# Self-attention of a decoder layer: GpSimd adds the last two keys' weighted values onto the first two, TensorE sums 14 terms per batch instead of 16

## The chip, the cores and the metric

One core of one Trainium2 chip runs the whole kernel. The metric is the device time of the kernel in microseconds (us). All times of the trace come from one profiled execution, and places in it are microseconds from the start of its span.

## The reference

One decoder layer over `x` of shape 32 x 128 x 128 (32 batches, 128 positions, D = 128): self-attention, cross-attention and a mixture of 8 experts of which each position takes two, each followed by a residual and a layer norm. The change touches the self-attention, whose 16 heads of 8 numbers attend to each other within one position:

```python
q = bitlinear(x, wq).reshape(B, S, H, Dh)      # k and v alike
scores = jnp.einsum('bshd,bstd->bsht', q, k) / Dh ** 0.5
attn = jax.nn.softmax(scores, axis=-1)         # over the 16 keys t of the same position
ctx = jnp.einsum('bsht,bstd->bshd', attn, v)
ctx = jnp.swapaxes(ctx, 1, 2).reshape(B, S, D)
return bitlinear(ctx, wo)
```

So a position has 16 x 16 scores, and its context is a sum over 16 keys of exponential times value, divided by the sum of the exponentials. `bitlinear` rounds its input to 8 bits after an rms norm and its weights to -1, 0, 1.

## The kernel before

**Stages.** The self-attention runs first, up to about 205 us; the cross-attention and the experts follow, and its last pieces (the output projection, residual and norm of the last tiles) run between the first pieces of the cross-attention. The self-attention takes one batch (128 positions on 128 partitions) per slot; four batches are a tile `u`, slots `j` = 0 to 3. `turns` writes out the slots of tiles 0 and 1, then a hardware loop over tiles 2 to 7 (two tiles a turn); the slots of the tail are written out by hand. Each engine runs its own list in a fixed order, and semaphores join the lists.

**One batch.** In slot `k` the engines work on different batches:

- TensorE multiplies batch k into `PS` with `w_pairs`, which holds for each pair of heads the sum of a query and a key weight, and into values. ScalarE squares the result into `pair_sq` (two buffers) and copies the values to `v1` (four buffers).
- VectorE's `pair_scores` reduces the squares of batch k-1 to scores, subtracts the key part and each head's largest, and writes `S1d` (lines 1962 to 1972). In slot 0 it does `largest_y` between the halves of this reduction, in slot 1 `y_scale` (`inv` and `s2`, lines 1948 and 1950), which waits for `clip2_ready` from GpSimd's `y_stats`.
- ScalarE's `exponentials` of batch k-2 (line 1449) writes the exponentials into the last 16 columns of each of the 16 key rows of `prod2` (two buffers of 16 x 144 floats; `TC` = 128 + 16). It waits for the scores and for the sum two batches before, which read the same buffer.
- GpSimd's `weigh` of batch k-2 (line 797) multiplies each key's exponentials with its values into the first 128 columns of that key's row, and raises `av_prod`.
- TensorE's `sum_keys` of batch k-3 (line 1033) adds the 16 rows of 144 columns in bank 6 of `PS`: 16 matmuls with the identity in fp32, which the trace shows as 32 passes. It waits for `av_prod` and for `hctx_ready` of the batch before, because the bank is single.
- VectorE's `context` of batch k-4 takes the reciprocal of the summed exponentials (line 1936) and scales the sum into `hctx` (line 1939), at the head of its slot, ahead of `pair_scores`. SyncE then stores `hctx` to `shuffle` and reads it back transposed into `Y`.

**Around it.** Per tile, GpSimd has three small pieces besides `weigh`, in this order: in slot 0, behind `weigh`, `y_stats` (lines 805 to 813: rms of `Y` and its clip); in slot 1, ahead of `weigh`, `y_rows` (lines 775 and 776), which waits for `s2` from `y_scale`; in slot 3, ahead of `weigh`, `first_scales` (lines 782 to 788), which waits for `mv1` from VectorE's `add_x` in slot 2. In tiles 0 and 1 it also centres expert weights (line 732) and takes powers of the rms of `x` (line 702). Its steps that read what it has just written wait on the engine's own chain counter (`ch`, `ch.settle`); `A_POOL_STEPS` says how many counted steps one turn of the loop makes.

**The tail.** GpSimd's list is `weigh(T, 0)`, `weigh(T, 1)`, `y_stats(T - 2)`, `prepare_pads` (lines 747 to 756), `y_rows(T - 2)` and then the first pieces of the cross-attention. ScalarE's `round_y(T - 2)` (line 1466 on) waits for `y_rows(T - 2)`. Between the two last weighs TensorE turns rows for the cross-attention (`turn_rows`, line 1127) behind a `sum_keys`, and ScalarE copies them (line 1584) before its last `exponentials`.

Of the kernel before, what the change touches and what calls it, by code (L numbers as in the profile page):

```python
# [8 lines left out]
def decoder_layer(nc, x, ctx_1024, mask, wq, wk, wv, wo, Wq, bq, Wk, bk, Wv, bv,  # L9
# [3 lines left out]
    ALU, ACT, AX = mybir.AluOpType, mybir.ActivationFunctionType, mybir.AxisListType  # L13

    B, P, D = x.shape
    H, HD = 16, D // 16
# [9 lines left out]
    NEG = -1e30  # L26
    ROUND = 1.5 * 2.0 ** 23
    A_STEPS = 66
    A_POOL_STEPS = 16
    EARLY = 4  # L30
    FULL = 5
    U = 2 * P
# [15 lines left out]
    with ctx:  # L48
        def sb(name, shape, dt=F32):
            return ctx.enter_context(nc.sbuf_tensor(name, shape, dt))  # L50
# [8 lines left out]
        def after(eng, s, n):  # L59

            eng.wait_ge(s, n + CREDIT)
# [127 lines left out]
        v1 = sb("v1", [P, 4, D])  # L189
        k2 = sb("k2", [P, H])  # L190

        SQ = H * H * HD + D
        TC = D + H
        pair_sq = sb("pair_sq", [P, 2, SQ])
        prod2 = sb("prod2", [P, 2, H * TC])
# [268 lines left out]
        def turns(eng, lag, slot, chain=None, steps=0):  # L464

            for u in range(lag):
                for j in range(TB):
                    one_slot(slot, u, j)  # L470
            with eng.Fori(0, (T - lag) // 2) as pair:
                if chain:
                    first = chain.n
                    chain.turn = pair * steps
                for v in range(2):
                    for j in range(TB):
                        slot(2 * pair + (lag + v), (lag + v) % 2, lambda l: True, j)
            if chain:
                made = chain.n - first
                assert made == steps, f"the loop makes {made} steps"  # L480
                chain.turn = 0
                chain.n += made * ((T - lag) // 2 - 1)
# [172 lines left out]
        def _(pool):  # L655
            ch = Chain(pool, pool_chain)
# [71 lines left out]
            def center_experts(n):  # L728

                c = slice(n * E * FC // 4, (n + 1) * E * FC // 4)  # L730
                pool.wait_ge(w_last_ready, 1)
                pool.tensor_tensor(W1_raw[:, c, 0:D - 1], W1_raw[:, c, 0:D - 1], bc(w_last[:, c], D - 1), ALU.subtract
                                   ).then_inc(w1_centered, 1)
# [56 lines left out]
            def weigh(u, j):  # L790

                k, i = TB * u + j, (j - 2) % TB
                after(pool, e1_ready, k - 1)
                rows = prod2[:, i % 2, :].rearrange("p (t c) -> p t c", c=TC)
                a = rows[:, :, D:TC].unsqueeze(2)
                v = v1[:, i, :].rearrange("p (t d a) -> p t d a", a=1, t=H)
                pool.tensor_tensor(rows[:, :, 0:D].rearrange("p t (d h) -> p t d h", d=HD),  # L797
                                   a.broadcast_to((P, H, HD, H)), v.broadcast_to((P, H, HD, H)), ALU.mult
                                   ).then_inc(av_prod, 1)

            def y_stats(t):
# [13 lines left out]
            def a_slot(u, parity, there, j):  # L815
                if j == 1 and there(2):
                    y_rows(u - 2)
                if j == 3 and there(2):
                    first_scales(u - 2)
                if there(-((j - 2) // TB)):  # L820
                    weigh(u, j)
                if isinstance(u, int) and (u, j) == (0, 2):
                    center_experts(2)
                if isinstance(u, int) and (u, j) == (0, 3):
                    center_router()
                    invert_rms(4, 2 * TB, 4 * TB)
                if isinstance(u, int) and (u, j) == (1, 0):
                    center_experts(3)
                if isinstance(u, int) and (u, j) == (1, 2):
                    invert_rms(7, 4 * TB, B)  # L830
                if j == 0 and there(2):
                    y_stats(u - 2)

            center_experts(0)
            center_experts(1)
            turns(pool, 2, a_slot, ch, A_POOL_STEPS)

# [29 lines left out]
            def b_slot(u, parity, there, j):  # L867
# [11 lines left out]
                if there(-l):  # L879
# [20 lines left out]
                    last.then_inc(split_ready, 1)  # L900

            weigh(T, 0)
            weigh(T, 1)
            y_stats(T - 2)
            prepare_pads()
# [47 lines left out]
            for j in range(NU):  # L953
# [6 lines left out]
                t, n = divmod(j - FIRST_FINAL + 1, FINAL_STEP)  # L960
                if 0 <= t < EARLY and n == 0:
                    center(t)
                t, n = divmod(j - FIRST_FINAL - 3, FINAL_STEP)
# [16 lines left out]
        def _(pe):  # L980
# [46 lines left out]
            def sum_keys(u, j):  # L1027

                k, i = TB * u + j, (j - 3) % TB
                after(pe, av_prod, k - 2)  # L1030
                after(pe, hctx_ready, k - 3)
                for t in range(H):
                    last = pe.matmul(PS[:, 6, 0:TC], ident[:], prod2[:, i % 2, TC * t:TC * (t + 1)],  # L1033
                                     start=(t == 0), stop=(t == H - 1))
                last.then_inc(hctx_psum, 1)

            def a_slot(u, parity, there, j):
# [39 lines left out]
                if there(-((j - 3) // TB)):  # L1077
                    sum_keys(u, j)
# [61 lines left out]
            def b_slot(u, parity, there, j):  # L1140
# [132 lines left out]
                if j == 0 and there(0):  # L1273
# [7 lines left out]
            pe.matmul(PS[:, 7, 0:2], w_square_top[:].broadcast_to((2, P)), ident[0:2, 0:2], start=True, stop=True  # L1281
                      ).then_inc(w_top_spread, 1)
            sum_keys(T, 0)
            turn_rows(0)
            expert(0)
            turn_context(0)
            expert(1)
            sum_keys(T, 1)
            one_slot(b_slot, 0, 1)
            expert(2)  # L1290
# [101 lines left out]
        def _(act):  # L1392
# [104 lines left out]
            def a_slot(u, parity, there, j):  # L1497
# [7 lines left out]
                if there(0):  # L1505
# [7 lines left out]
                    after(act, pair_psum, 2 * k + 2)  # L1513
                    act.activation(pair_sq[:, j % 2, 1024:SQ], PS[:].rearrange("p a b -> p (a b)")[:, 1024:SQ], ACT.Square  # L1514
                                   ).then_inc(pair_ready, 1)
# [971 lines left out]
```

## Time and profile before

| what | value |
|---|---|
| median of three runs | 676.63 us (676.59 to 677.73) |
| profiled execution | 676.38 us |
| its span, first to last instruction | 674.6 us |
| TensorE matmuls, busy | 532.8 us (79%) |
| VectorE, busy | 517.0 us (77%) |
| GpSimd, busy | 485.8 us (72%) |
| ScalarE, busy | 461.0 us (68%) |
| `sum_keys`, TensorE | 133.8 us in 1024 instructions |
| `weigh`, GpSimd | 117.5 us in 32 instructions |

The busy times are sums over the whole span, over stages with different limits. The profiled execution's time is 1.8 us more than its span; what lies outside the span is the same work before and after it. In the rows below an engine is named PE (TensorE), DVE (VectorE), ACT (ScalarE), POOL (GpSimd) or SP (SyncE); PEld is TensorE's weight load. Durations of a group are in ns, all else in us.

### The profile page before, as it was taken

Reading aid. Unit: us, or ns where it says so; the run is one execution under the profiler, and the core shown is the slowest. Engines: PE = TensorE matmul, PEld = TensorE weight load, DVE = VectorE, ACT = ScalarE, POOL = GpSimd, SP = SyncE. Lnnn points to the kernel's source line nnn. Section 1 sums busy time; section 2 is a strip of 40 time slices with the busy share of each in tenths; the row PEclk is TensorE's granted clock in tenths of the full one; section 3 lists DMA queues with packets and bytes.
Section 4 is the critical chain, followed back from the end, with each engine's and each line's share of the span. In section 5 each row is a group of like instructions: output and inputs, shape, how many; then the busy total and the mean of one; then the engine's idle time right before and its main releaser. Section 6 shows DMA issues by size and latency. Waiting matters only on the chain.

```text
span 674.6 us, 19683 instructions
## 1 busy us (share of the span) xinstructions
PE 532.8 (79%) x6500; PEld 434.0 (64%) x6500; DVE 517.0 (77%) x1549; ACT 461.0 (68%) x987; POOL 485.8 (72%) x668
## 2 busy tenths in 40 slices
PE   1699999999997477888798888888789999997100
PEld 0388878887887355656576666665578888886100
DVE  3888898889875667688768989888759666677584
ACT  4988898989865465777757777765445555677325
POOL 5798878887877465575678989984576776577553
PEclk9799999999999766999969999986789999999555
DMA  6922222221223343535301010000322433721332
GB/s 168 252 23 25 25 24 25 23 23 22 25 40 106 149 168 131 226 143 215 110 20 39 24 36 28 20 24 24 100 90 61 116 109 89 211 60 52 96 100 63
DMA packets 113108, 55.43 MB, mean 82 GB/s; under 512 B 70624, under 2 KB 103840, under 8 KB 113024
## 3 DMA queue, kind: packets, MB, share of 16 engines
q1 hardware_dynamic: 103984, 25.46, 17.2%
q10 hardware_dynamic: 4496, 19.02, 7.2%
q0 software_dynamic: 4544, 9.84, 4.2%
q8 instruction: 51, 0.84, 0.5%
q14 instruction: 33, 0.27, 0.1%
HBM read 21.25 MB, written 33.05 MB: 80 GB/s over the span
## 4 chain that ended last, share of the span: by engine, by line
PE 35%; DVE 19%; ACT 14%; issue 14%; POOL 11%; DMA 4%; DVEq 1%; SPq 1%; ACTq 0%; POOLq 0%
PE PS L1033 7%; PE PS L1144 3%; POOL prod L797 3%; PE PS L1243 3%; ACT W_raw L1624 3%; ACT prod L1632 3%; PE PS L1155 3%; POOL ys L924 3%; PE PS L1335 2%; PE PS L1352 2%; PE PS L1354 2%; PE PS L1337 2%; ACT X L1553 2%; PE PS L1336 2%; PE PS L1353 1%
## 5 line engine op out<-in xcount | busy, mean ns | idle before, releaser
L1033 PE MATMUL PS<-prod,ident 128*128 128x144 f32 x1024 | 133.8, 289 | 7.1 <-DVE hctx L1939 6.8
L1033 PEld LDWEIGHTS PS<-prod,ident 128*128 128x128 f32 x1024 | 128.0, 191 | 14.9 <-issue 9.6
L797 POOL TENSOR_TENSOR prod<-prod,v 128x2048 f32<-128x2048 f32 x32 | 117.5, 3673 | 13.9 <-ACT prod L1449 13.9
L924 POOL DMA_INDIRECT ys<-W_raw,ids x78 | 76.6, 982 | 31.2 <-issue 18.0
L2209 DVE TENSOR_REDUCE m<-PS 128x8 f32<-128x1024 f32 x64 | 77.8, 1216 | 27.0 <-PE PS L1155 26.9
L1155 PE MATMUL PS<-prod 49*128 49x128 bf16 x1024 | 66.5, 234 | 26.5 <-issue 12.8
L2318 DVE SCALAR_TENSOR_TENSOR W_raw<-PS,W_raw 128x512 f16<-128x512 f32 x78 | 52.3, 689 | 37.2 <-ACT W_raw L1689 37.2
L864 POOL DMA_INDIRECT xs<-Y,spot_u x64 | 64.0, 1000 | 22.9 <-issue 14.8
L1962 DVE TENSOR_REDUCE PS<-pair_sq 128x128 f32<-128x1024 f32 (+1 forms) x44 | 74.8, 1700 | 1.9 <-ACT pair_sq L1514 1.9
L1624 ACT ACTIVATE W_raw<-PS 128x1024 f32<-128x1024 f32 x64 | 65.8, 1028 | 13.0 <-PE PS L1160 13.0
L1155 PEld LDWEIGHTS PS<-prod 49*128 49x128 bf16 x1024 | 42.2, 101 | 46.2 <-issue 18.9
L892 POOL TENSOR_SCALAR pair_sq<-qk_rest 128x128 bf16<-128x128 f32 x128 | 66.8, 543 | 0.0
L1354 PE MATMUL PS<-W_lo,W_raw 128*128 x312 | 60.1, 222 | 0.0
L1353 PE MATMUL PS<-W_hi,W_raw 128*128 x312 | 59.9, 221 | 0.0
L1352 PE MATMUL PS<-W_hi,W_raw 128*128 x312 | 59.8, 221 | 0.0
L1689 ACT ACTIVATE W_raw<-PS 128x512 f16<-128x512 f32 x78 | 45.5, 596 | 11.3 <-PE PS L1337 9.4
L884 POOL TENSOR_TENSOR qk_rest<-qk_f,pair_sq 128x128 f32<-128x128 f32 x64 | 26.1, 431 | 37.6 <-ACT pair_sq L1613 37.2
L1612 ACT CAST pair_sq<-qk_f 128x384 bf16<-128x384 f32 x32 | 16.4, 512 | 52.5 <-DVE qk_f L2221 52.5
L1705 ACT ACTIVATE W_raw<-PS,w_rows 128x128 f32<-128x128 f32 x78 | 24.4, 364 | 39.4 <-PE PS L1354 37.2
L1243 PE MATMUL PS<-W_raw 128*32 128x128 f32 x1024 | 46.3, 304 | 3.2 <-issue 2.7
L1144 PE MATMUL PS<-ident,pair_sq 128*128 128x128 bf16 x512 | 43.4, 234 | 3.2 <-POOL pair_sq L896 2.2
L1335 PE MATMUL PS<-W_raw,W_hi 128*128 128x256 f16 x156 | 43.3, 278 | 1.5 <-issue 0.9
(319 smaller groups left out, 1540.6 us busy)
## 6 DMA issues: line engine op xcount, KB each, us to landing
xs<-pad ACTq DMA_DIRECT2D x16, 1152.0 KB, 4.6
Y<-xs SPq DMA_DIRECT2D x39, 144.0 KB
W_raw<-ys SPq DMA_DIRECT2D x16, 256.0 KB, 3.9
W_raw<-in_L_ffn_W_dram SPq DMA_DIRECT2D x1, 2048.0 KB
shuffle<-hctx SPq DMA_DIRECT2D x32, 64.0 KB, 3.0
Y<-shuffle SPq DMA_DIRECT2D x32, 64.0 KB, 1.7
cs<-in_ctx_dram SPq DMA_DIRECT2D x8, 256.0 KB, 3.1
out_dram<-W_raw SPq DMA_DIRECT2D x8, 256.0 KB, 2.3
```

Of the source, the lines that this page charges most:

```text
L797: pool.tensor_tensor(rows[:, :, 0:D].rearrange("p t (d h) -> p t d h", d=HD), a.broadcast_to((P, H, HD, H)), v.broadcast_to((P, H, HD, H)) ...
L892: ch(pool.tensor_scalar(slots(i, side, s, s + 1)[:, :, 0, :], heads(qk_rest[:, side]), 1.0, None, ALU.mult))
L924: pool.indirect_dma_start(ys[:], bass.IndirectOffsetOnAxis(ap=ids[:, j % KD, s:s + 1].bitcast(U32), axis=0), ou[j % OD][:, s, :], None).th ...
L1033: last = pe.matmul(PS[:, 6, 0:TC], ident[:], prod2[:, i % 2, TC * t:TC * (t + 1)], start=(t == 0), stop=(t == H - 1))
L1155: last = pe.matmul(PS[:, 2 * a + r, g * P:(g + 1) * P], left[rows, HG // 2 * a + g, :], right[rows, HG // 2 * a + g, :], start=True, stop= ...
L1243: last = pe.matmul(PS[HC * q:HC * (q + 1), 7, a * P:(a + 1) * P], head_frame(i % 2, h), PT[:, i % 2, h, :], start=(odd == 0), stop=(odd == 1))
L1352: pe.matmul(o, h_hi[j % 2][:, c, tokens], w_hi, start=False, stop=False)
L1353: pe.matmul(o, h_lo[j % 2][:, c, tokens], w_hi, start=False, stop=False)
L1354: last = pe.matmul(o, h_hi[j % 2][:, c, tokens], w_lo, start=False, stop=(c == FC - 1))
L1624: act.activation(half_heads(PT[:, i % 2], a), banks(a).rearrange("p r (g q) -> p r g q", q=P), ACT.Exp, scale=HD ** -0.5).then_inc(p_ready, 1)
L1962: step(dve.tensor_reduce(k2[:] if first == 2 * D else sums[:, first:end], pair_sq[:, i % 2, HD * first:HD * end].rearrange("p (c d) -> p c ...
L2209: dve.tensor_reduce(half_heads(m2[:], a), banks(a).rearrange("p r (g t) -> p r g t", t=P), AX.X, ALU.max).then_inc(max_done, 1)
```

## The change

`weigh` gets a second instruction. After the multiplication, and after a wait for it, GpSimd adds rows 14 and 15 of `prod2` (two keys' weighted values and their exponentials, 2 x 144 floats) onto rows 0 and 1 in place; `av_prod` is raised by this add. `sum_keys` then sums rows 0 to 13.

```diff
-    A_POOL_STEPS = 16
+    A_POOL_STEPS = 24
...
+        SUMMED = H - 2
...
-                pool.tensor_tensor(rows[:, :, 0:D].rearrange("p t (d h) -> p t d h", d=HD),
-                                   a.broadcast_to((P, H, HD, H)), v.broadcast_to((P, H, HD, H)), ALU.mult
+                ch(pool.tensor_tensor(rows[:, :, 0:D].rearrange("p t (d h) -> p t d h", d=HD),
+                                      a.broadcast_to((P, H, HD, H)), v.broadcast_to((P, H, HD, H)), ALU.mult))
+                ch.settle()
+                pool.tensor_tensor(rows[:, 0:H - SUMMED, :], rows[:, 0:H - SUMMED, :], rows[:, SUMMED:H, :], ALU.add
                                    ).then_inc(av_prod, 1)
...
-                for t in range(H):
+                for t in range(SUMMED):
                     last = pe.matmul(PS[:, 6, 0:TC], ident[:], prod2[:, i % 2, TC * t:TC * (t + 1)],
-                                     start=(t == 0), stop=(t == H - 1))
+                                     start=(t == 0), stop=(t == SUMMED - 1))
```

## Rows read from the trace of the kernel before

**Rows 1.** Busy time by stretch: stretch, its length, each engine, granted clock, DMA.

```profile
27.20:58.85 31.65, 29.99 (x204) 24.62 (x204) 28.12 (x59) 25.71 (x73) 31.25 (x15) 0.91 0.36 59
155.00:177.50 22.50, 21.17 (x161) 18.34 (x161) 20.08 (x47) 20.61 (x44) 18.29 (x16) 1.00 0.21 23
```

**Rows 2.** Timeline, VectorE in the loop: start, duration, line, operation, idle before and its releaser.

```profile
159.17 0.26 DVE L1936 RECIPROCAL E1inv<-PS 128x16 f32<-128x16 f32 x1 [0.26 <-PE PS L1033]
...
166.06 0.23 DVE L1936 RECIPROCAL E1inv<-PS 128x16 f32<-128x16 f32 x1
...
171.23 0.26 DVE L1936 RECIPROCAL E1inv<-PS 128x16 f32<-128x16 f32 x1 [0.57 <-PE PS L1033]
...
176.18 0.43 DVE L1972 TENSOR_TENSOR S1d<-PS,S1m 128x256 f32<-128x256 f32 x1
176.52 0.25 DVE L1936 RECIPROCAL E1inv<-PS 128x16 f32<-128x16 f32 x1
...
178.39 0.15 DVE L1948 TENSOR_REDUCE inv<-clips 128x4 f32<-128x8 f32 x1
...
181.02 0.42 DVE L1972 TENSOR_TENSOR S1d<-PS,S1m 128x256 f32<-128x256 f32 x1
181.69 0.26 DVE L1936 RECIPROCAL E1inv<-PS 128x16 f32<-128x16 f32 x1 [0.25 <-PE PS L1033]
```

**Rows 3.** Timeline, GpSimd in the loop.

```profile
166.22 0.20 POOL L782 TENSOR_TENSOR ve<-mv,norm_eps 128x4 f32<-128x4 f32 x1 [1.36 <-DVE mv L1997]
...
168.01 3.67 POOL L797 TENSOR_TENSOR prod<-prod,v 128x2048 f32<-128x2048 f32 x1
172.14 3.67 POOL L797 TENSOR_TENSOR prod<-prod,v 128x2048 f32<-128x2048 f32 x1 [0.45 <-ACT prod L1449]
175.76 0.21 POOL L805 TENSOR_TENSOR ms<-ssq,per_row 128x4 f32<-128x4 f32 x1
176.05 0.20 POOL L807 TENSOR_TENSOR ms<-ms,rms_eps 128x4 f32<-128x4 f32 x1
...
177.69 0.20 POOL L813 TENSOR_TENSOR clips<-clip,per_step 128x4 f32<-128x4 f32 x1
...
179.14 3.67 POOL L797 TENSOR_TENSOR prod<-prod,v 128x2048 f32<-128x2048 f32 x1
```

**Rows 4.** Timeline ahead of the loop: three of seven weighs, and `y_scale`.

```profile
27.19 3.67 POOL L797 TENSOR_TENSOR prod<-prod,v 128x2048 f32<-128x2048 f32 x1 [3.37 <-ACT prod L1449]
...
55.18 3.67 POOL L797 TENSOR_TENSOR prod<-prod,v 128x2048 f32<-128x2048 f32 x1
...
59.02 3.67 POOL L797 TENSOR_TENSOR prod<-prod,v 128x2048 f32<-128x2048 f32 x1 [0.17 <-ACT prod L1449]
...
65.72 0.15 DVE L1948 TENSOR_REDUCE inv<-clips 128x4 f32<-128x8 f32 x1
```

**Rows 5.** Timeline, one sum of the keys on TensorE.

```profile
167.03 4.16 PE L1033 MATMUL PS<-prod,ident 128*128 128x144 f32 x32 [0.82 <-DVE hctx L1939]
```

**Rows 6.** Single lines of the kernel: duration min/median/max in ns, first and last start.

```profile
L797 POOL TENSOR_TENSOR prod<-prod,v x32: 3666/3674/3685, 27.2 to 200.9; 128x2048 f32<-128x2048 f32 x32
...
L884 POOL TENSOR_TENSOR qk_rest<-qk_f,pair_sq x64: 415/428/448, 211.7 to 449.5; 128x128 f32<-128x128 f32 x64
...
L935 POOL TENSOR_TENSOR X<-X,bet x8: 1253/1262/1621, 591.0 to 658.4; 128x512 f32<-128x512 f32 x8
```

**Rows 7.** Timeline at the end of the self-attention.

```profile
190.53 3.67 POOL L797 TENSOR_TENSOR prod<-prod,v 128x2048 f32<-128x2048 f32 x1
...
194.92 4.19 PE L1033 MATMUL PS<-prod,ident 128*128 128x144 f32 x32
...
200.88 3.67 POOL L797 TENSOR_TENSOR prod<-prod,v 128x2048 f32<-128x2048 f32 x1 [2.62 <-ACT prod L1449]
...
211.79 0.19 ACT L1466 COPY spare_act<-round_up 128x1 f32<-128x1 f32 x1 [1.49 <-POOL rs L776]
```

## Prediction

> **What bounds the kernel now.** I read the windows by stage first, then the timeline of one turn of the self-attention loop engine by engine, then the groups by line for prices. In the loop every engine is nearly full: of 22.5 us (four batches) TensorE is busy 21.17, ScalarE 20.61, VectorE 20.08, GpSimd 18.29 [rows 1]. So no share decides; a cycle of waits does. VectorE's reciprocals, one a batch, come at 159.17, 166.06, 171.23, 176.52 and again at 181.69 [rows 2]: the loop takes 22.52 us per four batches. Two of them wait for `sum_keys` (0.57 and 0.25 us); the others start when VectorE's own work lets them. So TensorE is on the path only in part: without those waits VectorE alone would hold the loop at some 21.7 us. GpSimd has waits too, 1.36 us before `first_scales` and 0.45 us before a `weigh` [rows 3], and these look like slack.
>
> They are not all free. One loop goes twice through GpSimd in four batches: `weigh` (slot 3), `weigh` (slot 0), `y_stats`, VectorE's `y_scale`, the rest of that `pair_scores`, the next batch with `add_x`, `first_scales`, and `weigh` (slot 3) again. Its length today, from starts in [rows 2, 3]:
> - two weighs, start to next start (172.14 to 175.76): 2 x 3.62 = 7.24
> - `y_stats`, 175.76 to 177.89: 2.13; its word to VectorE 0.08, an estimate from the gaps of [rows 3]
> - `y_scale` at 178.39 to where the next reciprocal could start: S1d at 181.02 plus 0.34 (as 176.18 to 176.52) is 181.36: 2.97
> - 159.17 to 166.06: 6.89
> - 166.06 to `first_scales` at 166.22: 0.16; to `weigh` at 168.01: 1.79
>
> The sum is 7.24 + 14.02 = 21.26 us, so it has 1.26 us in hand against 22.52. Before the loop GpSimd is the bound itself: from 27.20 to 58.85 us it is busy 31.25 of 31.65 [rows 1], centring weights and raising rms to a power between six weighs, of which [rows 4] show the first and the last; the seventh (59.02) waits 0.17 us.
>
> **The change, part by part.**
>
> TensorE loses 2 of 16 terms. A sum is 32 recorded passes in 4.16 us [rows 5], 0.13 each; 4 passes fewer are 0.52 us per batch, and a sum takes 3.64. Over 32 batches that is 16.6 us of TensorE's time, and it counts only where the path waits for a sum.
>
> GpSimd gets one `tensor_tensor` add over 2 x 144 = 288 contiguous elements per batch, behind a wait for its own multiplication. The wait: in the chain of small operations one of 0.21 us at 175.76 is followed at 176.05, so 0.08 from end to start [rows 3], where unchained work starts 0.05 before the reported end (3.67 against 3.62). The add: no row has its size. The nearest are the subtraction of 128 elements (0.428) and the add of 512 (1.262) [rows 6]; on the line between them 288 elements take 0.428 + 160/384 x 0.834 = 0.78 us. The multiplication of 2048 in 3.674 would give less: with 0.2 us fixed (the four-element operations), 1.70 ns an element, 0.68 us; but one of its operands is the same element 16 times over, and the add of 512 has two full operands, as this one does. I take 0.78. The bounds are the two rows themselves: above 0.43 because it has more than 128 elements, below 1.26 because it has fewer than 512.
>
> The Trainium skill (GPSIMD Engine Reference, section "Elementwise — side-by-side cycle accounting") gives 4497 ns for an add of 2048 fp32 elements on GpSimd; the multiplication of that size here takes 3674 [rows 6], so the trace disagrees at that size, and agrees with the page's rate at 512. By the page's rate the add would be an estimate of 0.80 us and the end 0.4 us later than my sum.
>
> So one `weigh` costs a = 0.08 + 0.78 = 0.86 us more, 4.48 from start to next start. The multiplication's own writes, `v1`, the exponentials' columns (added with the rest, so the denominators are summed too) and the counts of semaphores stay in place; no DMA and no queue is touched. The larger number of steps per loop turn is only the count for the chain's waits: nothing. Behind the add on GpSimd's queue stand `y_stats`, `first_scales` and the next `weigh`; behind `av_prod` stands TensorE's sum. ScalarE's reuse of `v1` waits for a `weigh` two slots back and stays far behind it.
>
> The sum against the profiled execution, in three stretches:
> - Ramp. Seven weighs up to 59.02, each a late: 7 x 0.86 = 6.02. Two slacks go: 0.17 before the seventh, and, since `y_stats` would end at 59.02 + 3.62 + 2.13 and tell VectorE 0.08 later, at 64.85, while `y_scale` started at 65.72 [rows 4], 0.87. +4.98 us.
> - Loop. The cycle above becomes 2 x 4.48 + 14.02 = 22.98, +0.46 over 22.52. `y_scale` runs six times from 65.72 to 178.39, so five turns: +2.30. GpSimd's work alone would ask 4 x 4.48 + 2.13 + 0.08 + 0.75 (178.39 to 179.14) + 1.79 = 22.67, less; VectorE's and TensorE's own cycles are shorter still, so the 0.52 us buys nothing here.
> - Way out. From `y_scale` at 178.39: the 0.33 us (181.36 to 181.69) go; the `weigh` at 190.53 ends 0.86 later, its sum now starts as it ends (194.25, not 194.92, so 0.67 us of slack go) and is 0.52 shorter; it lets TensorE turn rows and ScalarE reach the last exponentials, whose `weigh` (200.88) waits for them [rows 7] and again costs 0.86. 1.72 - 1.52: +0.20.
>
> What follows is GpSimd's chain up to `y_rows`, for which ScalarE's rounding waits 1.49 us at 211.79 [rows 7], and the second attention behind that; lateness passes on. 4.98 + 2.30 + 0.20 = +7.5 us: 676.4 + 7.5 = 683.9 for the profiled execution. The median of the runs stands 0.25 above it: 684.1 us, 1.1% slower. The whole is 19a - 8.9, so it turns at a = 0.47 us; 0.1 us on the add moves the end by 1.9.
>
> **The rivals.**
>
> *TensorE was the bound and the add hides.* For it: TensorE is the busiest engine in [rows 1] and two reciprocals wait for it. VectorE's cycle would then hold: D from reciprocal to reciprocal of 4.84 (176.52 to 181.36), 6.89, 0.97 + 3.68 (166.06 to the sum at 167.03, then the shorter sum; [rows 2, 5]) and 5.29: 21.67 us, 0.85 less per turn. With a = 0.2 the ramp gives +0.4, five turns -4.3, the way out -1.1: 671.6 us. Against it: it needs a below 0.4, an add of 288 elements cheaper than one of 128 [rows 6]. It decides for faster from a = 0.40 down. Chance 0.06.
>
> *The two cancel.* With the add at the price of the 128-element row (a = 0.51) the ramp costs 2.5, the loop's cycle is 22.28 and gives back 1.2, the way out 0.5: +0.8, 677.4 us. Within 0.2% (about what a measurement of this kernel tells from no change, 1.35 us) for a from 0.40 to 0.54. For it: a fixed part of an operation could weigh more than I think. Chance 0.08.
>
> *Part of the lateness is taken up.* TensorE and ScalarE have waits of their own at the way out, and the shorter sums help wherever TensorE, not GpSimd, is late there. If half of the ramp is absorbed, 678.5 to 681.5. Against it: ScalarE waits for GpSimd by name at 211.79 [rows 7]. Chance 0.06.
>
> *The add runs slower beside VectorE.* One of the eight 512-element adds took 1.621 instead of 1.262 [rows 6]. At that ratio the add takes 1.00, a = 1.08: ramp +6.5; GpSimd alone is then the longer cycle, 4 x 4.70 + 4.75 = 23.55, five turns +5.2; way out +0.6: 689 us. Against it: the 32 multiplications lie within 3.666 to 3.685 while VectorE is nearly always busy. Chance 0.10, most of it for sizes between this and mine. The Trainium skill (GPSIMD Engine Reference, section "Specifications") says GpSimd's SBUF interface is shared with VectorE and contends with VectorE instructions that have two SBUF inputs; by that rule the time would go towards this 689, and the steady multiplications here do not bear it out.
>
> **How the numbers follow.** The forecast has the rest, 0.70; its own range is 681.5 to 686.5, from a of 0.73 to 0.98 (the multiplication's rate gives 682.2). From 679.5 to 687.5 I leave out the faster rival, the cancelling one, the top of the last and the bottom of the absorbed one, some 0.2. Faster 0.06, same 0.08, slower 0.86.
>
> **What would show it.** A new GpSimd group of 32 at about 0.78 us, starting 3.75 us after the multiplication; the sums' group with 14/16 of its instructions and 3.64 us per sum; TensorE's waits before a sum named after GpSimd, not after `hctx`. The seventh `weigh` near 64.0, the first `y_scale` near 70.7, the loop at 23.0 us per four batches, the last `y_scale` near 185.7, ScalarE's rounding near 219.3. GpSimd's wait before `first_scales` falls from 1.36 to some 0.2. I am wrong if the add is cheaper than 0.45, if the loop falls under 22.5, if the ramp's lateness is gone by the time of the second attention, or if TensorE's granted clock, 1.00 in [rows 1], falls with its lower load.

## The result, and the profile after

| kernel | median of the runs | range | runs |
|---|---|---|---|
| before | 676.50 us | 674.47 to 678.17 | 8 |
| changed | 681.24 us | 679.00 to 685.83 | 8 |

The ratio is 1.0076, 95% interval [1.0050, 1.0102]: the changed kernel is slower, by 4.7 us (3.4 to 6.9). The forecast was 684.1 us and slower; the time lies inside the range, below the forecast. The profiled execution of the changed kernel is the longest of its eight, 685.83 us with a span of 684.1; so the pair of profiles is 9.5 us apart, twice the medians' distance. The sections below therefore go by places inside the self-attention, which repeat, and treat what lies behind it by many runs.

The single lines of the changed kernel, duration min/median/max in ns and first and last start: the multiplication and the new add, each with the instructions that wait for it.

```profile
L798 POOL TENSOR_TENSOR prod<-prod,v x32: 3662/3672/3679, 26.7 to 208.6; 128x2048 f32<-128x2048 f32 x32
...
L801 POOL TENSOR_TENSOR prod<-prod x32: 791/796/803, 30.5 to 212.4; 128x288 f32<-128x288 f32 x32
  PE PS L1036: 15.2, 15
```

The add takes 796 ns, within 7 ns either way, and the multiplication has not changed. The line under it says who waits: TensorE's sum, 15.2 us in 15 waits. The page's group of the sums says the same in another way, busy us and mean ns of one, then the idle time before them, before and after:

```profile
L1033 PE MATMUL PS<-prod,ident 128*128 128x144 f32 x1024 | 133.8, 289 | 7.1 <-DVE hctx L1939 6.8
...
L1036 PE MATMUL PS<-prod,ident 128*128 128x144 f32 x896 | 122.1, 296 | 18.3 <-POOL prod L801 15.2
```

So TensorE did lose its work: 122.1 us in 896 instructions, where it had 133.8 in 1024. The chain of work that ended last, by engine, before and after, shows who took the path:

```profile
PE 35%; DVE 19%; ACT 14%; issue 14%; POOL 11%; DMA 4%; DVEq 1%; SPq 1%; ACTq 0%; POOLq 0%
...
POOL 40%; PE 23%; issue 13%; ACT 10%; DVE 8%; DMA 3%; SPq 1%; POOLq 0%; ACTq 0%; DVEq 0%
```

This line goes over the whole kernel and varies from execution to execution: a second profile of the changed kernel has GpSimd at 31% and TensorE at 22%. In both profiles `weigh` and its add make 18%, where `weigh` made 3% before. Now GpSimd's timeline in the loop, which answers to [rows 3]:

```profile
172.85 0.80 POOL L801 TENSOR_TENSOR prod<-prod 128x288 f32<-128x288 f32 x1
173.72 0.20 POOL L783 TENSOR_TENSOR ve<-mv,norm_eps 128x4 f32<-128x4 f32 x1
...
175.54 3.67 POOL L798 TENSOR_TENSOR prod<-prod,v 128x2048 f32<-128x2048 f32 x1
179.28 0.79 POOL L801 TENSOR_TENSOR prod<-prod 128x288 f32<-128x288 f32 x1
180.03 3.68 POOL L798 TENSOR_TENSOR prod<-prod,v 128x2048 f32<-128x2048 f32 x1
183.79 0.80 POOL L801 TENSOR_TENSOR prod<-prod 128x288 f32<-128x288 f32 x1
184.55 0.20 POOL L808 TENSOR_TENSOR ms<-ssq,per_row 128x4 f32<-128x4 f32 x1
```

One `weigh` goes from start to next start in 184.55 - 180.03 = 4.52 us, where it took 3.62. The add begins 3.74 and 3.76 us after its multiplication. `first_scales` had waited 1.36 us for VectorE. Now it starts at 173.72, 0.07 us behind the add's end and 0.08 behind the end of VectorE's `mv` (173.64), so that the two come almost together; in two other turns the profile still names a wait for `mv`, one of which is shown behind the end of `mv`:

```profile
173.36 0.28 DVE L2000 BATCH_NORM_AGGREGATE mv<-bn 128x2 f32<-128x6 f32 x3
...
196.73 0.20 POOL L783 TENSOR_TENSOR ve<-mv,norm_eps 128x4 f32<-128x4 f32 x1 [0.19 <-DVE mv L2000]
```

VectorE's `y_scale`, which started without a wait at 178.39 in [rows 2], now waits for GpSimd, as two of its turns show:

```profile
163.70 0.16 DVE L1951 TENSOR_REDUCE inv<-clips 128x4 f32<-128x8 f32 x1 [0.62 <-POOL clips L816]
...
186.73 0.16 DVE L1951 TENSOR_REDUCE inv<-clips 128x4 f32<-128x8 f32 x1 [0.81 <-POOL clips L816]
```

The turn takes 186.73 - 163.70 = 23.03 us; before it took 22.52. TensorE's timeline in the same turn shows where its shorter sums went:

```profile
169.20 3.70 PE L1036 MATMUL PS<-prod,ident 128*128 128x144 f32 x28 [0.38 <-POOL prod L801]
...
174.53 3.67 PE L1036 MATMUL PS<-prod,ident 128*128 128x144 f32 x28 [0.44 <-DVE hctx L1942]
...
180.21 3.69 PE L1036 MATMUL PS<-prod,ident 128*128 128x144 f32 x28 [1.04 <-POOL prod L801]
...
184.93 3.67 PE L1036 MATMUL PS<-prod,ident 128*128 128x144 f32 x28
```

A sum is 0.49 us shorter than in [rows 5], and what TensorE saves before 180.21 it then waits for the add (1.04). The windows of that turn (as [rows 1]: its length, then the busy time of TensorE, its weight loads, VectorE, ScalarE and GpSimd, granted clock, DMA) show GpSimd as the fullest engine, where TensorE was:

```profile
163.70:186.73 23.03, 19.66 (x148) 16.63 (x148) 20.22 (x47) 20.78 (x44) 21.47 (x19) 1.00 0.21 23
```

At the end of the self-attention the timeline shows GpSimd's `y_rows` and the rounding on ScalarE that waits for it, against 211.79 and 1.49 in [rows 7]; the first line is `y_rows` before:

```profile
211.56 0.20 POOL L776 TENSOR_TENSOR rs<-rms,s 128x4 f32<-128x4 f32 x1
...
220.20 0.20 POOL L777 TENSOR_TENSOR rs<-rms,s 128x4 f32<-128x4 f32 x1
...
220.44 0.19 ACT L1469 COPY spare_act<-round_up 128x1 f32<-128x1 f32 x1 [2.90 <-POOL rs L777]
```

The rounding is 8.65 us later. That is the loss of the self-attention, in one row.

### The profile page after: what moved, and what is told of

It reads as the page before. It is cut to its first block, busy times and chain, and to the rows that moved or that the text cites. A ratio compares the mean times of both kernels' runs of the same rounds, so it can differ in the third digit from the quotient of the medians.

```text
span 684.1 us, 19483 instructions
## 1 busy us (share of the span) xinstructions
PE 521.0 (76%) x6372; PEld 421.3 (62%) x6372; DVE 517.3 (76%) x1549; ACT 460.8 (67%) x987; POOL 513.7 (75%) x700
## 4 chain that ended last, share of the span: by engine, by line
POOL 40%; PE 23%; issue 13%; ACT 10%; DVE 8%; DMA 3%; SPq 1%; POOLq 0%; ACTq 0%; DVEq 0%
POOL prod L798 16%; POOL pair_sq L895 5%; POOL xs L867 4%; POOL ys L927 3%; PE PS L1338 2%; POOL prod L801 2%; PE PS L1355 2%; POOL qk_rest L887 2%; PE PS L1339 2%; PE PS L1340 2%; PE PS L1357 2%; POOL pair_sq L899 2%; PE PS L1356 2%; PE PS L1158 2%; PE PS L1147 2%
## 5 line engine op out<-in xcount | busy, mean ns | idle before, releaser
L1036 PE MATMUL PS<-prod,ident 128*128 128x144 f32 x896 | 122.1, 296 | 18.3 <-POOL prod L801 15.2
L1036 PEld LDWEIGHTS PS<-prod,ident 128*128 128x128 f32 x896 | 116.0, 196 | 27.1 <-issue 16.5
L1627 ACT ACTIVATE W_raw<-PS 128x1024 f32<-128x1024 f32 x64 | 65.8, 1028 | 11.8 <-PE PS L1163 11.7
L1357 PE MATMUL PS<-W_lo,W_raw 128*128 x312 | 58.7, 218 | 0.0
L1356 PE MATMUL PS<-W_hi,W_raw 128*128 x312 | 58.7, 219 | 0.0
L1355 PE MATMUL PS<-W_hi,W_raw 128*128 x312 | 58.6, 218 | 0.1
```

The costliest lines, as they stand in the source:

```text
L1355: pe.matmul(o, h_hi[j % 2][:, c, tokens], w_hi, start=False, stop=False)
L1356: pe.matmul(o, h_lo[j % 2][:, c, tokens], w_hi, start=False, stop=False)
L1357: last = pe.matmul(o, h_hi[j % 2][:, c, tokens], w_lo, start=False, stop=(c == FC - 1))
L1627: act.activation(half_heads(PT[:, i % 2], a), banks(a).rearrange("p r (g q) -> p r g q", q=P), ACT.Exp, scale=HD ** -0.5).then_inc(p_ready, 1)
```

## The experiments

The theory is that of the prediction: the add lengthens a loop that goes twice through GpSimd per turn and a ramp that GpSimd bounds alone, TensorE's saving buys nothing, and the lateness reaches the end. The rivals are that the changed sum or its waits on TensorE cost the time, and, once the end proved less late than the self-attention, that something behind takes lateness up. In the table "end of self-attention" is the second line of `y_rows` in the profiled execution, against 211.56 us in that of the kernel before; the ratio is against runs of the kernel before on the same chip (the first row as above; medians 674.83 us over 23 runs for the next four, 675.34 over 32 for the four behind them, 675.14 over 17 for the last three), and "measured" is the ratio turned into us. Another execution of the kernel before had `y_rows` at 211.98, so the fourth column is good to some 0.4 us.

| kernel | turn | median (runs) | end of self-attention | ratio, 95% interval | measured, us |
|---|---|---|---|---|---|
| changed, first comparison | 23.03 | 681.24 (8) | +8.6 | 1.0076 [1.0050, 1.0102] | +3.4 to +6.9 |
| changed, again | 23.0 | 680.29 (12) | +8.6 | 1.0069 [1.0041, 1.0098] | +2.8 to +6.6 |
| 14 terms, no add | 21.69 | 665.43 (6) | -5.2 | 0.9863 [0.9825, 0.9900] | -11.8 to -6.7 |
| add, 16 terms | 23.03 | 682.93 (6) | +8.2 | 1.0126 [1.0090, 1.0162] | +6.1 to +10.9 |
| one slot, 13 terms | 22.1 | 673.20 (12) | -2.6 | 0.9974 [0.9945, 1.0002] | -3.7 to +0.1 |
| ramp only | 22.5 | 680.88 (8) | +5.6 | 1.0078 [1.0053, 1.0104] | +3.6 to +7.0 |
| loop only | 23.0 | 678.49 (12) | +3.0 | 1.0029 [1.0004, 1.0054] | +0.3 to +3.6 |
| tail only | 22.5 | 678.54 (12) | +0.8 | 1.0045 [1.0024, 1.0065] | +1.6 to +4.4 |
| before, again | 22.5 | 675.63 (12) | +0.4 | 1.0012 [0.9990, 1.0035] | -0.7 to +2.4 |
| before, 16 fills | 22.5 | 685.96 (6) | +10.3 | 1.0157 [1.0118, 1.0196] | +8.0 to +13.2 |
| before, 9 fills | 22.5 | 683.90 (6) | +5.6 | 1.0149 [1.0107, 1.0191] | +7.2 to +12.9 |
| slots 2 and 0 | 22.05, mean of five | 671.67 (12) | -3.1 | 0.9945 [0.9919, 0.9971] | -5.5 to -2.0 |

**The changed kernel again**, unaltered, on the chip of the next three.

> The changed kernel unaltered, for a second profile beside the first. In the first, ScalarE's rounding behind the last weigh (y_rows) comes some 8.6 us later than before, but the whole is 9.5 us longer in that one profile and only 4.7 in the median of the runs. Theory (the lateness is all made in the self-attention): y_rows again near 220.2 us, within 0.5, and what differs between executions lies behind it. Rival (the self-attention itself varies): y_rows between 215 and 221.

`y_rows` comes at 220.21 us, 0.01 from the first profile: within the self-attention the loss repeats. The total is 5.5 us longer than the kernel before, again less than the 8.6 there.

**The shorter sum without the add.** The kernel before, with one edit in `sum_keys`, which leaves two keys out of the sum; GpSimd's list is untouched.

```diff
-                for t in range(H):
+                for t in range(SUMMED):
```

> TensorE sums 14 terms and GpSimd adds nothing (two keys are left out of the sum). Theory (VectorE's cycle bounds the loop once TensorE is shorter): 21.7 us per four batches, 0.85 less, nothing gained ahead of the loop where GpSimd is the bound; 4.3 us over five turns and 0.5 at the way out, about 671.7 us. Rival (TensorE is the bound): 0.52 us in each of 32 batches, 16.6 less, 660 us. Second rival (TensorE's sums are hidden): 676.5, unchanged.

The loop takes 21.69 us, as VectorE's own cycle in the prediction (21.67). VectorE's timeline shows why no more can be had from TensorE: the two reciprocals of a turn that waited in [rows 2] (0.25 and 0.57 us) wait no longer (155.76 and 167.32), and from `y_scale` to `y_scale` it is 174.48 - 152.79 = 21.69.

```profile
152.79 0.15 DVE L1949 TENSOR_REDUCE inv<-clips 128x4 f32<-128x8 f32 x1
...
155.76 0.25 DVE L1937 RECIPROCAL E1inv<-PS 128x16 f32<-128x16 f32 x1
...
167.32 0.26 DVE L1937 RECIPROCAL E1inv<-PS 128x16 f32<-128x16 f32 x1
...
174.48 0.15 DVE L1949 TENSOR_REDUCE inv<-clips 128x4 f32<-128x8 f32 x1
```

So the saving on TensorE is worth something by itself, 0.83 us a turn, and it is the add that takes it away. At `y_rows` the kernel is 5.2 us early, where 4.8 was expected; its median is 9.4 us below, so 4 us more come from behind `y_rows`, which was not expected.

**The add with 16 terms.** The changed kernel; the add's result goes to a tile not in use and the sum keeps its 16 terms.

```diff
-                pool.tensor_tensor(rows[:, 0:H - SUMMED, :],
+                pool.tensor_tensor(att2[:].rearrange("p a b -> p (a b)")[:, 0:2 * TC].rearrange("p (t c) -> p t c", c=TC),
                                    rows[:, 0:H - SUMMED, :], rows[:, SUMMED:H, :], ALU.add
...
-                for t in range(SUMMED):
+                for t in range(H):
```

> GpSimd makes the same add, into a buffer that nobody reads, and TensorE sums all 16 terms. Theory (the add alone makes the time, the shorter sums are worth nothing beside it): the loop stays at 23.0 to 23.1 us per four batches, y_rows at most 0.6 us later than in the changed kernel, the time as that one's, 681 to 682. Rival (the shorter sums gave back most of what the add cost): 0.52 us per batch come on top, some 12 to 16 us, 693 or more.

VectorE's timeline, two turns of `y_scale`:

```profile
162.76 0.16 DVE L1951 TENSOR_REDUCE inv<-clips 128x4 f32<-128x8 f32 x1 [0.31 <-POOL clips L816]
...
185.79 0.16 DVE L1951 TENSOR_REDUCE inv<-clips 128x4 f32<-128x8 f32 x1 [0.33 <-POOL clips L816]
```

The turn is 23.03 us with 16 terms as with 14. Beside the add, two terms fewer buy nothing in the loop; the rival that puts the loss on the changed sum falls, since here TensorE's list is that of the kernel before. TensorE's waits for the add are still there in this kernel; in the changed one they reach VectorE as 0.33 us before one reciprocal of the turn (183.94), and `y_scale` behind it then waits 0.81 us for GpSimd all the same. At the end of the kernel the median is 2.6 us above that of the changed one, though `y_rows` comes 0.4 us sooner; the two intervals overlap.

**One part at a time.** A condition in `weigh` and `sum_keys` decides for which batches the add is made; the others go as before. "Ramp only" folds five of the seven batches of the ramp; the last two count as the loop's. Each of the three kernels has one of the `return` lines.

```diff
+        def folded(u, j):
+            return isinstance(u, int) and TB * u + j < 7                         # ramp only
+            return not isinstance(u, int) or 7 <= TB * u + j < TB * T            # loop only
+            return isinstance(u, int) and u >= T                                 # tail only
```

> Add and 14 terms only for the five batches weighed ahead of the loop's pattern (tiles 0 and 1), 16 terms elsewhere. Theory: five adds of 0.88 us less 1.04 of slack, first y_scale 3.3 us later than before (69.0), loop back at 22.5 us per four batches, nothing caught up, y_rows near 214.9. Rival (the loop catches up, since GpSimd has waits in it): y_rows back near 211.6. What lies behind y_rows took 461 to 462 us in the median of before and 458 to 459 in the changed kernel: with the theory of lateness alone it is 461 to 462 here; if shorter sums ahead of the loop do it, 458 to 459.

> Add and 14 terms only for the batches weighed from the end of tile 1 to tile 7. Theory: first y_scale 0.7 us later, loop at 23.0 us per four batches, y_rows 2.6 us later than before, near 214.2. Rival (the loop's cycle is made by what the ramp leaves behind): loop at 22.5, y_rows near 212. Behind y_rows: 461 to 462 us if the terms do not matter there, 458 to 459 if the lower load of TensorE in the loop does.

> Add and 14 terms only for the last two batches, weighed behind the loop. Theory: one add of 0.88 us shows, y_rows near 212.4. Behind y_rows: 461 to 462 us if nothing there depends on the terms, 458 to 459 if the shorter last sums let TensorE start the cross-attention's preparation sooner.

At the end of the self-attention the three are late by 5.6, 3.0 and 0.8 us, together 9.3 where the whole is 8.6. Loop and tail are as expected (214.5 for 214.2; 212.4). The ramp is 2.2 us above what was expected of it. TensorE's timeline in the ramp-only kernel shows most of that miss, one sum that takes 5.85 us beside one of the usual 4.16:

```profile
63.34 5.85 PE L1046 MATMUL PS<-prod,ident 128*128 128x144 f32 x32 [2.15 <-POOL prod L803]
...
70.25 4.16 PE L1046 MATMUL PS<-prod,ident 128*128 128x144 f32 x32
```

and its windows over that sum show the granted clock (third number from the end) under full speed:

```profile
63.30:66.30 3.00, 2.96 (x15) 2.97 (x16) 2.93 (x6) 3.00 (x5) 3.00 (x1) 0.62 0.34 27
66.30:69.30 3.00, 3.00 (x21) 2.86 (x21) 0.54 (x3) 0.11 (x2) 2.31 (x6) 0.81 0.08 22
```

The reciprocal behind that sum waits 2.34 us for it.

**Only a later start.** To see whether the stage behind takes lateness up whatever its cause, the kernel before got fills of an unused tile on GpSimd, at one place early in the ramp, and nothing else.

```diff
+                    for _ in range(16):        # the other kernel: 9
+                        ch(pool.memset(att2[:], 0.0))
+                        ch.settle()
```

> The kernel before with 16 idle fills (0.6 us each) on GpSimd in tile 0, all sums of 16 terms: a pure lateness of some 8.6 us, no add. Theory (lateness made ahead of the loop is never caught up): y_rows near 220.2. Rival: part is caught up in the loop, where GpSimd has waits; y_rows below 218. Behind y_rows the median of before is 461.5 to 462 us and that of the changed kernel 458 to 459: if the later start alone shortens what follows, 458 to 459 here and 681 in all; if not, 461 to 462 and 684.

> The same with 9 fills, a lateness of some 4.4 us: y_rows near 216, 679.5 to 680 us in all if what follows takes as long as before; less if a later start shortens it.

They come 1.7 and 1.1 us later to `y_rows` than expected, again with a slow sum (5.97 and 5.77 us long, at a granted clock of 0.69 and 0.72, after waits of 9.21 and 4.68 us for GpSimd). Neither is taken up behind: 10.3 us at `y_rows` are 8.0 to 13.2 at the end, and 5.6 are 7.2 to 12.9, even more. A later start is not made good by itself.

**The kernel before again**, with its own profile, to see how one kernel varies.

> The kernel before, for a second profile. If its self-attention is the same in every execution, y_rows comes at 211.6 within 0.3 us again, and what follows takes other than 463 us (the median of its runs asks for 461 to 462). If the self-attention varies, y_rows moves by a microsecond or more.

The windows from `y_rows` to the end of the span, for the kernel before as first profiled,

```profile
211.56:674.60 463.04, 351.94 (x5177) 280.12 (x5175) 342.61 (x1154) 287.93 (x593) 314.22 (x500) 0.87 0.28 93
```

for the same kernel in this run,

```profile
211.98:669.30 457.32, 343.50 (x5177) 273.67 (x5175) 341.40 (x1154) 288.08 (x593) 314.14 (x500) 0.89 0.28 94
```

and for the changed kernel as first profiled:

```profile
220.20:684.10 463.90, 351.04 (x5173) 279.44 (x5173) 341.78 (x1151) 287.70 (x593) 316.87 (x500) 0.87 0.28 92
```

The same instructions of the same kernel take 463.0 us at a mean granted clock of 0.87 and 457.3 at 0.89, and 8.4 of TensorE's busy time are gone in the second. A pair of single executions cannot tell whether lateness is taken up there; the 9.5 us between the first two profiles is that kind of pair.

**Where the add costs less.** Two kernels make the add only in slots whose cycle has room. The first folds three keys in slot 2 of the loop and nowhere else, the second three keys in slot 2 and one in slot 0.

```diff
+        def folded(u, j):                      # one slot, 13 terms
+            return j == 2 and not (isinstance(u, int) and u < 2)
...
+        def folded(u, j):                      # slots 2 and 0: keys to fold
+            return {2: 3, 0: 1}.get(j, 0) if not isinstance(u, int) else 0
```

> The add only where the theory sees slack on GpSimd: in slot 2 of tiles 2 to 7 (three keys onto three, an add of 432 elements, about 1.1 us), TensorE sums 13 terms there and 16 elsewhere. Theory: the long cycle through GpSimd does not hold this weigh, the sum in slot 3 is 0.78 shorter and lets VectorE start 0.66 earlier; loop at 21.9 us per four batches, 3.3 to 4 us less than before, 672.5 to 673.5. Rival (any add on GpSimd lengthens the loop): six adds of 1.1 us, up to 7 later, 683.

> In the loop only: three keys added in slot 2 (13 terms summed) and one key in slot 0 (15 terms). Theory: the long cycle through GpSimd carries one add of 144 elements, 0.53 us, 21.26 + 0.53 = 21.8; the cycle from the weigh in slot 3 through the sums comes to 21.95 and governs: six turns of 0.55 us less, y_rows near 208.2, time 3.4 below before. Rival (the add in slot 0 costs what it cost in the changed kernel): loop at 22.4 or more, y_rows 210 or later.

Both shorten the turn, to 22.1 and, over five turns, 22.05 us, where 21.9 and 21.95 were expected; at `y_rows` the first is 2.6 us early, where 3.3 to 4 were expected, the second 3.1, where 3.4 were. TensorE's timeline of the first shows the cycle that comes next: the 13-term sum is quick, but the full sum of the next batch starts behind its own `weigh` (the release named), and VectorE's next reciprocal, at 174.48, waits for it.

```profile
165.33 3.42 PE L1046 MATMUL PS<-prod,ident 128*128 128x144 f32 x26 [0.46 <-DVE hctx L1952]
...
170.26 4.18 PE L1046 MATMUL PS<-prod,ident 128*128 128x144 f32 x32 [0.53 <-POOL prod L803]
```

GpSimd's timeline of the second kernel, its two adds, of 432 and of 144 elements:

```profile
163.34 1.10 POOL L810 TENSOR_TENSOR prod<-prod 128x432 f32<-128x432 f32 x1
...
173.59 0.49 POOL L810 TENSOR_TENSOR prod<-prod 128x144 f32<-128x144 f32 x1
```

This second kernel is faster than the kernel before, at 0.9945 [0.9919, 0.9971] of its time; for the first the interval, 0.9974 [0.9945, 1.0002], just reaches no change.

## Why the prediction was right, and where its sizes were off

**a = 0.86 us.** Right: 4.52 - 3.62 = 0.90 in the loop. The add, put between the rows of 128 and 512 elements [rows 6] at 0.78, takes 0.796; the wait ahead of it is 0.07 to 0.08. The adds of 144 and 432 elements (0.49, 1.10) lie on one line with it, some 0.18 us plus 2.1 ns an element, which also gives the 1.26 of 512. The rivals that needed a cheap add (below 0.54 us a `weigh`) fall with this row, and so does the add at 1.00 us beside VectorE: 791 to 803 ns in all 32. VectorE was busy 20.22 of a turn's 23.03 us all the while. The Trainium skill (GPSIMD Engine Reference, section "Specifications") says that GpSimd shares its SBUF interface with VectorE and contends with VectorE instructions that have two SBUF inputs. No row of this loop shows such a slowing.

**Loop: 22.98 us.** Right in size and in mechanism: 23.03, 23.03 with 16 terms too, and 21.69 with the add gone. Both links of the cycle that goes twice through `weigh` can be seen: VectorE's wait for `clips`, and `first_scales`, which starts 0.08 us behind the end of `mv` in five of six turns. With the measured 4.52 us the cycle comes to 2 x 4.52 + 14.02 = 23.06. But it is the longest by little: GpSimd's own list, with all four weighs of a turn, comes to 4 x 4.52 + 4.75 = 22.83 by the prediction's terms, and the profile's chain of work follows that list through all four. So of the 0.51 us that the turn grew, GpSimd's list alone would account for 0.31; that the other cycle sets the last 0.2 is read from the trace, and no run parts the two. Over five turns it cost 2.95 us by the first and the last `y_scale` (71.11 and 186.73, where 65.72 and 178.39 stood), forecast 2.30: four turns took 23.00 to 23.03, and one, from 94.12, took 23.55. It is the only one of the five in which a `weigh` waits for ScalarE's exponentials, and ScalarE is busy 22.22 us in it:

```profile
100.17 3.68 POOL L798 TENSOR_TENSOR prod<-prod,v 128x2048 f32<-128x2048 f32 x1 [0.74 <-ACT prod L1452]
```

**Ramp: +4.98 us.** Right in mechanism, too small by 0.4: the first `y_scale` came at 71.11. From the first to the seventh `weigh` (26.74 to 63.61) it is 36.87 us, where it was 31.83: 5.04 more, for 4.99 in the prediction's terms. The seventh is early, not late (forecast near 64.0), because the first began 0.45 us sooner in this execution. The extra arises behind it: GpSimd's word could have come at 68.11 + 2.13 + 0.08 = 70.32, but `y_scale` starts 0.79 us later and without a wait for it. TensorE's timeline shows the cause, a sum that is slow beside the first full-speed one:

```profile
63.78 5.36 PE L1036 MATMUL PS<-prod,ident 128*128 128x144 f32 x28 [3.03 <-POOL prod L801]
...
70.21 3.67 PE L1036 MATMUL PS<-prod,ident 128*128 128x144 f32 x28
```

It is 1.69 us longer than the other, with the clock at 0.69 and 0.74 (below), and VectorE's reciprocal waits 2.72 us for it. In the kernel with the add and 16 terms the clock stayed at 1.00 there, and `y_scale` comes, behind a wait for GpSimd, 4.97 us later than before, as forecast; the lines are GpSimd's and VectorE's of the changed kernel, then VectorE's of that one:

```profile
26.74 3.67 POOL L798 TENSOR_TENSOR prod<-prod,v 128x2048 f32<-128x2048 f32 x1 [2.93 <-ACT prod L1452]
...
63.61 3.67 POOL L798 TENSOR_TENSOR prod<-prod,v 128x2048 f32<-128x2048 f32 x1
...
71.11 0.15 DVE L1951 TENSOR_REDUCE inv<-clips 128x4 f32<-128x8 f32 x1
...
70.69 0.16 DVE L1951 TENSOR_REDUCE inv<-clips 128x4 f32<-128x8 f32 x1 [0.26 <-POOL clips L816]
```

So the changed kernel's +5.39 is the forecast's cost, less an earlier start, plus a slow sum that the forecast did not have. The prediction named a falling clock among what would make it wrong, but only in the loop, where it stayed at 1.00.

**Way out: +0.20 us.** Right within 0.11: from the last `y_scale` to the rounding it is 33.71 us for 33.40. Up to the last `weigh` 0.60 us are gained (forecast 0.66), behind it 0.91 are lost (0.86). With ramp and loop that makes 8.65 at the rounding, where 7.5 was forecast (+5.39, +2.95 and +0.31 for 4.98, 2.30 and 0.20).

**Lateness passes on.** This is the step that did not hold in full: +8.6 at the end of the self-attention are 3.4 to 6.9 and 2.8 to 6.6 us at the end of the kernel. Of the table's rows, the kernels with the add and 16 terms, with one slot, with the ramp, with the loop, with 16 fills and with slots 2 and 0 have the shift at `y_rows` inside the measured interval. Four kernels have not: the changed one and 14 terms without the add end 3 to 4 us earlier than their shift, the tail alone and 9 fills 2 and 3 to 4 us later. So on the whole a shift passes on one for one, with a scatter of a few us to either side that is more than the intervals allow. What makes it stays open. It is not the later start as such (16 and 9 fills); not ramp, loop or tail alone, none of which ends early; not the code behind, which is the same. The two edits that end early are those with 14 terms in all batches, but why this should be worth 3 to 4 us behind `y_rows` no run shows.

The granted clock goes with a part of the scatter. Over all 13 profiles the stretch from `y_rows` to the end of the span takes 457.3 us (the kernel before, again) to 465.3 us (ramp only), and TensorE is busy 343.5 and 356.0 us in these two; over the 13 the two figures rise together (correlation 0.86). Over the runs of the kernel before, a clock lower by 0.01 in the mean of a run goes with some 2 us more. The 9 fills ran at a median clock of 0.903, where the kernel before beside them had 0.913, and 14 terms without the add at 0.917, beside 0.911: by an estimate from these figures, 2 us of the one's lateness and 1 us of the other's gain. For the changed kernel, 0.913 beside 0.911, it explains next to nothing, and why the clock differs was not tested.

"Part of the lateness is taken up", one of the rivals with 0.06, forecast 678.5 to 681.5, and the median lies in it; its mechanism, waits at the way out of the self-attention that shorter sums fill, is refuted by the same trace, where that stretch costs 0.3 us more, not less. The forecast's own range, 681.5 to 686.5, missed the median by 0.3, the wide one held it. That it did is in part luck: the self-attention came 1.2 us later than forecast, and the stretch behind it was some 4 us shorter for a reason that the prediction does not have.

## What to carry to other kernels

When an instruction is lengthened to relieve a fuller engine, follow the loops of waits and count how often each goes through it: here one loop went twice through `weigh` and GpSimd's own list four times, so that 0.9 us on GpSimd cost a turn of the loop 0.51 us, while TensorE's 0.5 us a batch, without the add, gained it only 0.83. Put the extra work first in the slots that such a loop does not pass, elsewhere keep it well below what the loop has in hand, and keep it out of a ramp where the engine is the bound by itself. The version that gained clearly put 1.10 us in slot 2, which the loop does not pass, and 0.49 us in slot 0, which it does; with slot 2 alone the gain is not clear of noise. A shift read in one pair of traces holds as far as the stage repeats: behind it, compare medians of many runs before a cause is sought.

## What the runs showed of the hardware

TensorE's granted clock fell after GpSimd had made it wait, in five of the six profiles with a long wait of this kind in the ramp (2.06 to 9.21 us). In the changed kernel TensorE stands idle for 3.03 us ahead of the sum at 63.78 (its row is above); the windows around it:

```profile
57.00:60.00 3.00, 3.00 (x25) 2.79 (x24) 2.83 (x8) 1.44 (x2) 3.00 (x2) 1.00 0.29 30
60.00:63.30 3.30, 0.75 (x4) 0.20 (x2) 2.92 (x10) 2.52 (x10) 3.22 (x2) 1.00 0.08 12
63.30:66.30 3.00, 2.52 (x13) 2.52 (x14) 2.81 (x6) 2.68 (x5) 3.00 (x2) 0.69 0.28 24
66.30:69.30 3.00, 3.00 (x19) 2.86 (x18) 0.28 (x2) 0.01 (x1) 2.77 (x5) 0.74 0.08 22
69.30:75.00 5.70, 4.86 (x38) 4.02 (x36) 5.05 (x13) 5.20 (x10) 4.10 (x6) 1.00 0.19 16
```

TensorE is busy 3.00 us of 3.00, then 0.75 of 3.30, and when it takes up work again the clock is 0.69 and 0.74 over two windows, part of each at 1.2 GHz, before it is back at 1.00 (2.4 GHz). In the kernel with the add and 16 terms a wait of 2.06 us at the same place left the clock at 1.00 and the sum at 4.18 us; TensorE had been busy 2.13 us from 60.00 to 63.30 there. With the ramp alone, a wait of 2.15 us, in a stretch with 1.13 us busy, was followed by the fall. The two kernels with fills show it too, and there nothing but a delay on GpSimd was put in. A wait caused by GpSimd could thus cost a second time, as a slower sum behind it.
